# A Perceiver block on one core: softmax numerators as bytes, rotary halves exchanged by DMA, the first two split scales taken together

## The reference

```python
q = fq_sym((layernorm(x) @ Wq + bq) / sqrt(32))      # 16 heads of 32, int8 per query row
k = fq_sym(context @ Wk + bk)                        # int8 per key
v = fq_sym(context @ Wv + bv)                        # int8 per channel over all 4096 keys
a = softmax(q @ k.T); s = max(a) / 255; a = clip(round(a / s), 0, 255) * s
x = x + (a @ v) @ Wp + bp
# latent attention: 16 heads of 128, with q and k each extended by 64 rotary columns:
#   rope(u) = u * cos + concat(-u2, u1) * sin,  u1, u2 the halves of the 64
x = x + mla(layernorm(x))
x = x + ffn(layernorm(x))                            # ternary weights, int8 rows, Hadamard transform of 2048
```

## Time and profile before

| | before |
|---|---|
| three runs | 595.64, 595.75, 596.13 us; median 595.75 |
| the profiled execution's own time | 594.12 us |
| its span, first to last instruction | 592.3 us |
| busy, PE / PEld | 535.1 / 339.2 us |
| busy, DVE / ACT / POOL | 452.5 / 364.0 / 36.0 us |
| mean granted TensorE clock | 0.976 of full |
| DMA moved | 76.81 MB |

### The profile page before, as it was taken

How to read it: one execution, slowest core, us unless ns; L and a number is a source line. 1 busy time by engine, 2 the same in 40 slices (tenths; PEclk the granted TensorE clock), 3 DMA queues, 4 the chain that set the end, 5 groups by cost and what they waited for, 6 DMA issues and landing times. The chain is left out here.

```text
span 592.3 us, 10689 instructions
## 1 busy us (share of the span) xinstructions
PE 535.1 (90%) x4315; PEld 339.2 (57%) x4318; DVE 452.5 (76%) x846; ACT 364.0 (61%) x428; POOL 36.0 (6%) x32
## 2 busy tenths in 40 slices
PE   1999999998899999989996897799998899994996
PEld 1444555543566656656665665588884556551483
DVE  2699999966899989998998895211663886787794
ACT  4624556454899889988997897102126455638443
POOL 0300000000200200020006000000000000001300
PEclk9999999999999999999998899799999999996999
DMA  8623300052254535544437489200605805020000
GB/s 319 254 72 95 119 1 1 0 181 66 109 184 157 182 94 172 196 144 141 146 112 300 143 284 427 95 0 1 283 1 212 368 1 212 2 71 1 1 2 35
DMA packets 18897, 76.81 MB, mean 130 GB/s; under 512 B 1952, under 2 KB 3104, under 8 KB 16800
## 3 DMA queue, kind: packets, MB, share of 16 engines
q1 hardware_dynamic: 18848, 76.13, 35.8%
HBM read 75.34 MB, written 0.79 MB: 129 GB/s over the span
## 5 line engine op out<-in xcount | busy, mean ns | idle before, releaser
L1090 DVE CUSTOM_DVE_ANT_0 arena<-ps,arena 128x1024 f32<-128x1024 f32 x128 | 152.5, 1220 | 15.1 <-issue 6.8
L1475 ACT ACTIVATE arena<-arena,small 128x4096 int16<-128x4096 f32 x32 | 121.6, 3798 | 2.4 <-DVE small L1103 2.4
L578 PE MATMUL ps<-arena 128*128 128x512 f16 x384 | 100.1, 380 | 0.0
L619 PE MATMUL ps<-small,arena 128*128 128x128 bf16 x1024 | 81.0, 224 | 8.5 <-DVE arena L1110 4.9
L544 PE MATMUL ps<-arena 128*128 128x512 f16 x384 | 85.2, 379 | 1.0 <-DVE arena L1021 1.0
L619 PEld LDWEIGHTS ps<-small,arena 128*128 128x128 bf16 x1024 | 60.8, 100 | 18.0 <-issue 6.9
L780 PE MATMUL ps<-arena 128*128 128x256 f32 (+1 forms) x288 | 68.7, 397 | 1.4 <-ACT arena L1558 1.4
L1482 ACT ACTIVATE arena<-ps 128x512 int32<-128x512 int32 x96 | 56.9, 593 | 20.4 <-PE ps L619 20.1
L780 PEld LDWEIGHTS ps<-arena 128*128 128x128 f32 x288 | 55.7, 194 | 12.6 <-issue 3.3
L544 PEld LDWEIGHTS ps<-arena 128*128 128x128 f16 x384 | 37.1, 98 | 43.6 <-issue 1.3
L635 PEld LDWEIGHTS ps<-arena 128*128 128x128 f16 x1024 | 42.7, 97 | 29.0 <-issue 6.5
(11 more groups left out here) (164 smaller groups left out, 742.4 us busy)
## 6 DMA issues: line engine op xcount, KB each, us to landing
arena<-key_scales SPq DMA_DIRECT2D x64, 512.0 KB, 5.1
arena<-in_ctxT SPq DMA_DIRECT2D x8, 1024.0 KB, 5.6
arena<-in_wg SPq DMA_DIRECT2D x1, 4096.0 KB, 12.0
arena<-in_wo SPq DMA_DIRECT2D x1, 4096.0 KB, 12.5
arena<-in_wu SPq DMA_DIRECT2D x1, 4096.0 KB, 21.9
arena<-in_wd SPq DMA_DIRECT2D x4, 1024.0 KB, 6.5
arena<-in_wuq SPq DMA_DIRECT2D x1, 3072.0 KB, 24.4
arena<-in_wkr SPq DMA_DIRECT2D x1, 2048.0 KB, 13.6
```

What stands on the lines that cost most here:

```text
L578: last = pe.matmul(ps[:, bank, :], wv16[wpart][:, k, g * P:(g + 1) * P], ctx16[cpart][:, k, tok], start=(k == 0 and i == 0), stop=(k == KC ...
L619: last = pe.transpose(ps[:, bank, :].bitcast(BF16)[:, b * P:(b + 1) * P], p16[u % 2][:, (8 * q + b) * P:(8 * q + b + 1) * P].bitcast(BF16) ...
L1090: dve.tensor_tensor_reduce(sc[:, u % 2, i * SCW:(i + 1) * SCW], ps[:, 2 * (n % 2):2 * (n % 2) + 2, :].rearrange("p a b -> p (a b)"), skb[: ...
L1475: act.activation(p16[u % 2], sc[:, u % 2, :], ACT.Exp, bias=ebias[:, u % 2:u % 2 + 1], scale=sq[:, i:i + 1], accum_out=rsum[:, u:u + 1]).t ...
```

## The change

Four things change.

1. **Bytes.** The exponentials are written as bytes, key k of block 2m beside key k of block 2m+1. Two neighbouring bytes are one 16-bit word, so TensorE turns 16 blocks per unit instead of 32, in two halves. ScalarE stores half 0 and VectorE half 1 as 1024 words each, into the score buffer's second quarter. GpSimd takes the words apart in four parts, from bytes to f16 numbers, into pT; for this it waits for the stored words and for the products of the unit before. VectorE's fourth score quarter of the unit after next waits until all is taken apart. The exponential's bias moves from VectorE to ScalarE, just ahead of the exponential. A value quarter moves from ScalarE to VectorE. GpSimd's rounding of values is woven into its unpacking, and the output weights' scaling and the residual's bias come behind the unpacking of units 27 and 28.
2. **Rotary.** TensorE's eight rotations and the matrix's load are gone; the sign is in the sine table. SP issues four DMAs behind job 5 (keys) and four behind job 9 (queries) that copy the raw blocks with halves exchanged, 32 partitions each. ScalarE's first magnitude sum waits for all ropes, as its scratch lies over the exchanged queries.
3. **Start.** VectorE takes the three scale steps of extents 0 and 1 before its loop; TensorE turns the latents before spread_max(0); ScalarE takes bound(1) before it stores the latents.
4. The factor 2^24 is gone.

```diff
@@ tiles
-        p16 = [at(o_sc + 4 * M * b, [M], I16) for b in range(2)]
+        p8 = [at(o_sc + 4 * M * b, [M], U8) for b in range(2)]
+        p_pairs = [at(o_sc + 4 * M * b + 4 * SCW, [M], U8) for b in range(2)]
+        p_words = [at(o_sc + 4 * M * b + 4 * SCW, [M // 2], I16) for b in range(2)]
...
@@ sync
+            for i, (raw, turned, steps) in enumerate(((krT, turned_k, QR0 // 2), (qrT, turned_q, UK0 // 2))):
+                sp.wait_ge(pja, steps)
+                sp.wait_ge(pjd, steps)
+                for a in range(0, P, DR // 2):
+                    b = a ^ (DR // 2)
+                    sp.dma_start(turned[a:a + DR // 2], raw[b:b + DR // 2]).then_inc(ld_turn[i], 16)
...
@@ tensor
-            def turn_p(u, q):
+            def turn_p(u, half):
...
+                    m = 8 * half + b
                     last = pe.transpose(ps[:, bank, :].bitcast(BF16)[:, b * P:(b + 1) * P],
-                                        p16[u % 2][:, (8 * q + b) * P:(8 * q + b + 1) * P].bitcast(BF16), idb[:, :])
+                                        p8[u % 2][:, 2 * m * P:2 * (m + 1) * P].bitcast(BF16), idb[:, :])
...
-                pe.wait_ge(*pT_stored(u, q))
+                pe.wait_ge(unp, NCH * u + q + 1)
...
-            spread_max(0)
             turn_latents()
+            spread_max(0)
             spread_max(1)
...
-                if late:
-                    turn_p(s - 2, 2)
...
-                if late:
-                    turn_p(s - 2, 3)
...
-                r = rope_after(n)
-                if r is not None:
...
@@ vector
                     elif k >= 2:
-                        dve.wait_ge(tp, NCH * (u - 2) + 2 * (k - 1))
+                        if k == 2:
+                            dve.wait_ge(tp, 2 * (u - 1))
+                        else:
+                            dve.wait_ge(unp, NCH * (u - 1))
...
+            for e in range(2):
+                split_max(e)
+                split_guard(e)
+                split_inverse(e)
...
                 if s >= 3:
                     store_out(s - 3)
+                if late:
+                    store_pairs(s - 2, 1)
                 if now:
                     scale_scores(s, 0)
...
-                if late:
-                    store_pT(s - 2, 2)
...
-                if half == 0:
-                    store_values(group, 0)
+                if half is not None:
+                    store_values(group, 3 * half)
                 if now:
                     scale_scores(s, 3)
...
-                if now:
-                    exp_bias(s)
...
@@ gpsimd
+            def unpack(u, q):
+                pool.wait_ge(*pairs_stored(u, q // 2))
+                if u:
+                    pool.wait_ge(pv, NCH * (u - 1) + q + 1)
+                pool.tensor_copy(pT[:, 8 * q:8 * q + 8, :].rearrange("p (m e) a -> p m e a", e=2),
+                                 p_pairs[u % 2][:, q * SCW:(q + 1) * SCW].rearrange(
+                                     "p (m a e) -> p m e a", m=4, e=2)).then_inc(unp, 1)
...
+            for s in range(UNITS + 1):
+                group, half = values_turned_in(s)
+                if half == 0:
+                    round_values(group, 0)
+                    round_values(group, 1)
+                for q in range(NCH):
+                    if s:
+                        unpack(s - 1, q)
+                    if half == 0 and q in (1, 2):
+                        round_values(group, q + 1)
+                if s == FIRST_OUT + 1:
+                    scale_output_weights()
+                if s == FIRST_OUT + 2:
+                    bias_residual()
...
@@ scalar
             def exponentials(u):
...
+                act.activation(ebias[:, u % 2:u % 2 + 1], mfin[:, u % 2:u % 2 + 1], ACT.Identity, scale=nsq[:, i:i + 1],
+                               bias=ln255[:, 0:1]).then_inc(eb, 1)
                 act.wait_ge(eb, u + 1)
-                act.activation(p16[u % 2], sc[:, u % 2, :], ACT.Exp, bias=ebias[:, u % 2:u % 2 + 1],
+                act.activation(p8[u % 2].rearrange("p (m k e) -> p m e k", k=P, e=2),
+                               sc[:, u % 2, :].rearrange("p (m e k) -> p m e k", e=2, k=P), ACT.Exp,
+                               bias=ebias[:, u % 2:u % 2 + 1],
                                scale=sq[:, i:i + 1], accum_out=rsum[:, u:u + 1]).then_inc(ex, 1)
...
+            def store_pairs(u, half):
+                act.wait_ge(tp, 2 * u + half + 1)
+                act.activation(p_words[u % 2][:, half * SCW:(half + 1) * SCW],
+                               ps[:, turn_bank["p", u, half], :].bitcast(I16), ACT.Copy).then_inc(tact, 1)
...
             bound(0)
+            bound(1)
             store_latents()
-            bound(1)
...
-                if 0 <= s - 2 < UNITS:
-                    store_pT(s - 2, 3)
-                if half == 1:
-                    store_values(group, 3)
                 if prev:
-                    store_pT(s - 1, 0)
+                    store_pairs(s - 1, 0)
                 if s:
                     for g, j, bank in steps:
                         store_projected_values(g, j, bank)
                 if half == 0 and group:
                     store_values(group, 1)
-                if prev:
-                    store_pT(s - 1, 1)
...
                     act.wait_ge(ld_g, 16)
+                    if n == V0 - 2:
+                        act.wait_ge(rpu, NROPE)
```

More of the change, by code:

```diff
@@ L157, in build @@
         exp_table = small([1])
+        ln255 = small([1])
         ps = es.enter_context(nc.psum_tensor("ps", [P, 8, 512], F32))
@@ L229, in build @@
         rtmp = at(rest + 8192, [2, N])
-        rot_sb = at(rest + 10240, [P])
+        turned_k = at(rest, [NH // 2, N])
+        turned_q = at(rest + 15872, [NH // 2, N])
         ones = at(rest + 10752, [P])
@@ L389, in turns @@
             g, half = values_turned_in(s)
-            out = [("p", s - 2, 2)]
+            out = []
             if half == 1:
-                out.append(("v", g, 2))
-            out.append(("p", s - 2, 3))
-            out += [("v", g, 3)] if half == 1 else [("v", g, 0)] if half == 0 and g else []
+                out += [("v", g, 2), ("v", g, 3)]
+            if half == 0 and g:
+                out.append(("v", g, 0))
             out.append(("p", s - 1, 0))
@@ L782, in _ @@
                 last.then_inc(pj, 1)
-                r = rope_after(n)
-                if r is not None:
-                    pe.wait_ge(pjd if r % 2 else pja, (KR0 + r) // 2 + 1)
-                    if r >= 2:
-                        pe.wait_ge(rpu, r - 1)
-                    for b in range(2):
-                        last = pe.matmul(ps[:, 6 + r % 2, b * N:(b + 1) * N], rot_sb, rope_raw(r)[:, b, :],
-                                         start=True, stop=True)
-                    last.then_inc(rp, 1)
             pe.wait_ge(pja, NJ // 2)
@@ L1380, in _, with round_values @@
             bias_queries()
-            for g in range(G):
+            def round_values(g, c):
                 pool.wait_ge(vscale, g + 1)
-                for c in range(NCH):
-                    part = slice(c * SCW, (c + 1) * SCW)
-                    pool.tensor_scalar(v32[:, part], v32[:, part], vinv[:, g:g + 1], MAGIC, ALU.mult,
-                                       ALU.add).then_inc(vint, 1)
-            pool.wait_ge(ld_wp, 32)
-            pool.wait_ge(ld_xr, 16)
-            for g in range(G):
-                pool.tensor_scalar(wp_sb[:, g, :], wp_sb[:, g, :], sv[:, g:g + 1], 0.0, ALU.mult, ALU.add).then_inc(wpp, 1)
@@ L1393, in _ @@
-            for t in range(QT):
-                pool.tensor_tensor(xr[:, t, :], xr[:, t, :], bp_sb, ALU.add).then_inc(xrb, 1)
+                part = slice(c * SCW, (c + 1) * SCW)
+                pool.tensor_scalar(v32[:, part], v32[:, part], vinv[:, g:g + 1], MAGIC, ALU.mult,
+                                   ALU.add).then_inc(vint, 1)
+            def unpack(u, q):
[5 more added lines that the diff above has]
+                                     "p (m a e) -> p m e a", m=4, e=2)).then_inc(unp, 1)
@@ new lines, in scale_output_weights, with bias_residual @@
+            def scale_output_weights():
+                pool.wait_ge(ld_wp, 32)
+                for g in range(G):
+                    pool.tensor_scalar(wp_sb[:, g, :], wp_sb[:, g, :], sv[:, g:g + 1], 0.0, ALU.mult, ALU.add).then_inc(wpp, 1)
+            def bias_residual():
+                pool.wait_ge(ld_xr, 16)
+                for t in range(QT):
+                    pool.tensor_tensor(xr[:, t, :], xr[:, t, :], bp_sb, ALU.add).then_inc(xrb, 1)
+            for s in range(UNITS + 1):
+                group, half = values_turned_in(s)
+                if half == 0:
+                    round_values(group, 0)
[9 more added lines that the diff above has]
+                    bias_residual()
@@ L1656, in constants @@
     sin = np.concatenate([np.sin(ang)] * 4, -1).astype(f).T
-    rotate = np.zeros((P, P), f)
-    for m in range(P):
```

(5 more changed lines are left out.)

92 lines of the change are left out of this document (44 added, 48 removed).

## The result

The changed kernel's median is **601.22 us** (9 runs, 597.73 to 603.73), that of the kernel before in the same comparison 596.54 us (9 runs, 595.64 to 598.32): a ratio of 1.0067, 95% interval 1.0041 to 1.0094. It is slower by 0.7%. The changed kernel's times spread over 6.0 us, those of before over 2.7 here and over as much in a later comparison of 17 runs (594.29 to 600.35).

A forecast was written before the change was run, and what follows sets the result against it. The prediction saw TensorE, VectorE and ScalarE at their limit together in ordinary attention slots. Its terms summed to +0.65 us on the profiled 594.12; with the median 1.63 above that, it forecast 596.4 us, range 587 to 607.

The forecast's parts named there:

- ordinary slots: Attention-loop slots with value projection: ScalarE's chain takes 6.68 us against 6.45, times 18, +4.1 us.
- pairs: Pairs of attention-loop slots that turn a finished value group: a middle one takes 16.6 us against 17.19; together -3.4 us.
- last five: Last five attention-loop intervals: TensorE waits for scaled output weights behind unpackings; +4.2 us, with 0.7 for the clock.
- tail: Last exponential's end to last output scaling: the chain with unpacking takes 6.65 us against 3.83, +2.8 us.
- rotary: Query projection stretch: eight rotations leave TensorE (-6.9 us), but the first weight sum waits for rope; -5.85 us arrive.
- start: Kernel start to key projection: latents stored earlier, query projection from 13.3 us instead of 14.98; -1.2 us.
- all behind it: From the second attention's first scores on: the forecast had no term here, 0 us.
- rivals A: Attention loop: GpSimd's unpacking binds above 1.42 us each; at 1.3 604 us, at 1.5 613; chance 0.25.
- the byte half of D: Attention loop: byte output slows the exponential by 10%, 0.38 us a unit, +12 us; 608 us; whole rival's chance 0.08.
- its other half: Rotary stretch: the DMA exchange of halves is late; 608 us; whole rival's chance 0.08.
- B's cheap unpacking: Attention loop and tail: unpacking takes 0.85 us, giving 590 us; chance 0.27, shared with pairs recovering their idle time.

The follow-up runs named there:

- bias_dve: The changed kernel with the exponential's bias computed on VectorE again: 596.58 us, ratio 1.0012.
- split_exp: The changed kernel with each exponential split into two instructions of 2048 elements, their two sums added on VectorE: 597.44 us, ratio 1.0026.
- rotary_only: The kernel before with only the exchange of rotary halves by DMAs: 591.46 us, ratio 0.9917.
- start_only: The kernel before with only the start part of the change: 594.39 us, ratio 0.9972.
- rotary_start: The kernel before with the change's rotary and start parts, without its byte part: 588.16 us, ratio 0.987.
- bytes_only: The changed kernel with the old rotation and the old start, so only the byte part remains: 607.96 us, ratio 1.0192.
- mended: The changed kernel with the bias on VectorE, each exponential in two halves and the output weights scaled earlier: 599.71 us, ratio 1.0066.

## Why the prediction came out as it did

The forecast was 596.4 us, no change (within 1.2 us); the kernel is slower by 0.7%, 4.7 us, which lies within the range of 587 to 607 and outside what the forecast calls no change. By its own terms, on the profiled executions (forecast, then measured):

| term | forecast | measured |
|---|---|---|
| ordinary slots | +4.1 | +2.7 |
| pairs | -3.4 | -0.6 |
| last five | +4.2 | +8.2 |
| tail | +2.8 | +2.5 |
| rotary | -5.85 | -4.8 |
| start | -1.2 | -1.45 |
| all behind it | 0 | +1.4 |

The measured ones sum to +8.0.

**Last five, the step that failed most.** The mechanism was right: a wait for the first scaled weight (about 3 us forecast, 2.43 found), with the next unit's turn queued behind it. The mis-sized part is "TensorE idles more, and I add 0.7 (0 to 3)" for the clock. The output projections, 1.12 us for two at the high level and 2.08 at the low one, lie between the exponential's end and the turn, and the experiments put some 2.35 us of clock on one interval alone. The last of the five also grew from 6.46 to 8.16, with ScalarE waiting 2.93 us for turns behind such projections.

**Pairs.** For the middle pairs the order was counted right where the clock held: 16.63 against the 16.6 worked out. But the second pair fell to 0.90 and gave +0.6 in place of -0.6, and the last, at 0.70 for 0.81, kept 0.3 of 1.3. The first was worth -0.3 and not -0.9 at a clock of 1.00, so there the order was counted wrong: its first slot grew from 11.32 to 12.62, and `bias_dve` takes 1.06 off this pair, so much of the miss is the bias in ScalarE's chain. "A pair with TensorE busy 15.18 of 17.19 us kept 1.00, so I charge ordinary slots nothing" held for the changed kernel's ordinary slots (1.00 in all three stretches) and not for its pairs; in `bias_dve` an ordinary slot fell too (8.20 us at 0.79). That the clock could suffer outside the last five was said there from the Trainium skill, TensorE: Matmul & The Clock Gate (Part 1), by which inactivity brings the low clock, and weighed at nothing. This trace agrees in so far as the low level came where TensorE had gaps: in the last five and in the two stretches at 0.50 behind the loop. It does not tell why one middle pair fell to 0.90 and the other, with the same work, kept 1.00.

**Ordinary slots.** ScalarE is the limit, as argued; 6.61 for 6.68 because the idle time was 0.71 for 0.76. The bias took its 0.38, the exponential kept 3.80 with byte output, and the copies their 1.02 and 0.77. `bias_dve` and `split_exp` confirm the chain by taking either link out. Unpacking at 1.04 (1.1 forecast) stays off it, so rivals A and the byte half of D fell; the exchanges were in time, so its other half fell too. B's cheap unpacking (0.85) did not come.

**Tail, rotary, start.** 10.26 us from the last exponential's start to the last output scaling, against 7.72: +2.5. The rotary step was right to 0.03 us over its own stretch, -5.88; 1.1 of it was lost before, at the low level behind the loop. `rotary_only` shows the step alone: 30.40 us from the copy to the first scores, -5.87, and nothing lost before the copy. Its median gain of 4.5 us has an interval of about 3.7 to 6.3, which leaves room for 5.85. The key projection starts at 23.04 for 23.79, near the forecast (22.8), and the first exponential at 138.22 for 139.67. One profile does not fix this -1.45: the first exponential came between 137.53 and 140.06 in the eleven profiled kernels with the new start, and between 139.67 and 140.61 in the three with the old one. The surer figure is the -1.8 of `start_only` (0.7 to 2.6).

**Behind the first scores** no cost was forecast, and 1.4 us came. In the 20 us from these scores on the granted clock was 0.91 in the changed kernel, in `rotary_only`, `rotary_start` and `start_only`, which all lose 1.4 to 1.9 us behind this point; before and `bytes_only` have 1.00 there, and `bytes_only` loses 0.1. So the loss goes with the clock and the bytes do not bring it; what does stays open, with one profile of each kernel.

The sign went wrong because the terms nearly cancelled: +11 and -10.5. An error of 4 us in one of them was enough, and the clock entered the last five, the pairs, the rotary stretch and what lies behind it.

## What to carry to other kernels

When several engines are full together, moving work off one helps only if the chain that then ends last gets no longer: here moving one 0.38 us instruction back off that chain gave 4.6 of the 4.7 us. Price each part of a composite change by itself and keep the parts that pay; here two of three did, and they are worth 1.3%. Where work leaves TensorE, cost every chain that still runs through it at the low level of its clock as well, and widen the range by that.

## What the runs showed of the hardware

GpSimd turns 1024 bytes a partition into 16-bit floats, with a stride of two in its input, in 1.04 us, four in 4.00, beside a VectorE busy 6.34 of 6.61 us. ScalarE writes bytes in an interleaved order as fast as 16-bit words in sequence (3.80 us for 4096 elements), and an instruction over one element with scale and bias from memory takes 0.38 us. Halving an exponential costs 0.5 us: from its start to the end of the last accumulator read 4.41 us (301.22 to 305.63 in `split_exp`) for 3.90. Copying 1024 16-bit words from PSUM takes 1.02 us on ScalarE and 0.69 on VectorE. And a pair of slots with 13.6 us of TensorE's work at the high level took 16.63 us at a granted clock of 1.00 and 17.81 at 0.90; in `mended`, with its two edits to the pair, it took 19.53 at 0.83, where kernels with one of them take 16.8 at 1.00.
